# Attention passes of a graph network: columns of gathered rows made by ScalarE and TensorE out of a transposed table in SBUF

## The reference, cut to what matters

```python
h = (x @ W).reshape(-1, heads, out_ch)
alpha_s = (h * a_s[None]).sum(-1)
alpha_d = (h * a_d[None]).sum(-1)
e = alpha_s[src] + alpha_d[dst]          # the first also adds a term of edge_attr_8
e = jnp.where(e > 0, e, NEG_SLOPE * e)
w = jnp.exp(e - segment_max(e, dst)[dst])
out = segment_sum(w[:, :, None] * h[src], dst) / segment_sum(w, dst)
```

## Time and profile before

| | |
|---|---|
| median of the runs | 13222.6 us |
| span of the profiled execution | 13211.9 us |
| GpSimd busy | 9802.5 us (74%) |
| VectorE busy | 6811.8 us (52%) |
| ScalarE busy | 4061.7 us (31%) |
| TensorE busy | 517.1 us (4%) |

### The profile page before, as it was taken

How to read it: one execution, slowest core, us unless ns; L and a number is a source line. 1 busy time by engine, 2 the same in 40 slices (tenths; PEclk the granted TensorE clock), 3 DMA queues, 4 the chain that set the end, 5 groups by cost and what they waited for, 6 DMA issues and landing times. The chain is left out here.

```text
span 13211.9 us, 103483 instructions
## 1 busy us (share of the span) xinstructions
PE 517.1 (4%) x1768; PEld 338.5 (3%) x1768; DVE 6811.8 (52%) x10645; ACT 4061.7 (31%) x4014; POOL 9802.5 (74%) x10362
## 2 busy tenths in 40 slices
PE   3000001100000200000010000000000000000001
PEld 1000000100000200000000000000000000000000
DVE  2777876377777533333333333343333336656656
ACT  4333333233333311111111111111111113666663
POOL 7777776777777677777777777777777776777775
PEclk9999999555555655555555555555555555555555
DMA  8445444344444222222212222222222223444443
GB/s 334 120 123 129 123 123 107 90 123 123 123 122 124 64 66 65 63 65 66 63 45 61 61 63 62 60 49 58 62 61 61 61 63 89 160 160 156 162 160 116
DMA packets 977609, 1316.81 MB, mean 100 GB/s; under 512 B 660939, under 2 KB 676770, under 8 KB 963551
## 3 DMA queue, kind: packets, MB, share of 16 engines
q10 hardware_dynamic: 558595, 803.76, 18.8%
q0 software_dynamic: 334400, 373.85, 14.8%
q1 hardware_dynamic: 83996, 134.02, 2.8%
HBM read 651.23 MB, written 659.53 MB: 99 GB/s over the span
## 5 line engine op out<-in xcount | busy, mean ns | idle before, releaser
L1862 POOL DMA_INDIRECT c_y<-g_tab,srcs x4545 | 4291.3, 944 | 1386.9 <-issue 1386.9
L2318 POOL DMA_INDIRECT c_y<-h_tab,srcs x1547 | 1461.0, 944 | 506.4 <-issue 471.4
L824 POOL DMA_INDIRECT c_y<-h_tab,srcs x1531 | 1444.9, 944 | 467.1 <-issue 467.1
L824 POOL DMA_INDIRECT first_y<-h_tab,srcs x1452 | 1370.6, 944 | 445.2 <-issue 442.6
L1894 DVE TENSOR_TENSOR c_s<-c_y,c_ad 128x64 f32<-128x64 f32 x300 | 79.6, 265 | 1905.2 <-DMA c_y<-g_tab,srcs 1873.7
L1979 ACT ACTIVATE c_ex<-c_de 128x64 f32<-128x64 f32 x300 | 67.9, 226 | 3171.7 <-issue 2847.4
L1930 DVE COPY c_w_in<-c_ex 128x64 f32<-128x64 f32 x300 | 66.8, 223 | 1580.1 <-ACT c_ex L1979 1580.1
L1938 DVE TENSOR_TENSOR_SCAN c_acc<-c_r,c_w_in 128x1156 f32<-128x1156 f32 x300 | 753.9, 2513 | 10.4
L846 DVE TENSOR_TENSOR_SCAN c_q_all<-c_mask,c_q_in 128x408 f32<-128x408 f32 (+2 forms) x800 | 734.3, 986 | 16.3 <-issue 8.8
L890 DVE TENSOR_TENSOR_SCAN c_acc<-c_r,c_w_in 128x408 f32<-128x408 f32 (+2 forms) x800 | 732.0, 978 | 6.9
L939 ACT ACTIVATE c_q_in<-c_q_raw 128x1552 f32<-128x1552 f32 (+1 forms) x200 | 596.7, 2983 | 271.8 <-DVE c_q_in L906 197.5
(11 more groups left out here) (405 smaller groups left out, 6432.2 us busy)
## 6 DMA issues: line engine op xcount, KB each, us to landing
c_y<-g_tab SPq DMA_DIRECT2D x12288, 0.3 KB
rows_d<-c_row ACTq DMA_DIRECT2D x96, 2048.0 KB, 6.9
rows_d<-c_row ACTq DMA_DIRECT2D x288, 576.0 KB, 2.9
c_q_raw<-q_start ACTq DMA_DIRECT2D x194, 776.0 KB, 6.2
rows_d<-c_row ACTq DMA_DIRECT2D x192, 784.0 KB, 4.3
c_y<-h_tab SPq DMA_DIRECT2D x6144, 0.2 KB
c_y<-g_tab ACTq DMA_DIRECT2D x6144, 0.3 KB
q_start<-first_y SPq DMA_DIRECT2D x97, 776.0 KB, 8.9
```

Source lines behind the costliest of these rows:

```text
L824: nc.gpsimd.indirect_dma_start(y[:, g % NY, k, 0:D], None, h_tab, source(g, k))\
L1862: nc.gpsimd.indirect_dma_start(y[:, g % NY, k, :], None, g_tab, source(g, k))\
L2318: nc.gpsimd.indirect_dma_start(y[:, g % NY, k, :], None, h_tab, source(g, k))\
```

## The change

In the three attention passes ScalarE sends no single-row DMAs any more. Instead:

- The pass keeps `h` in SBUF turned: `turn_pairs` transposes it on TensorE two nodes of a partition at a time, `copy_pairs` writes it back over `h`. Column (pair, partition) then holds the 64 features of two neighbouring nodes.
- `scalar_part` copies, edge by edge, the column of an edge's source pair to a column of `xs`: 128 ScalarE copies of 128x1 for a column of `y`, in four parts of 32, the place of each read from registers. Two 16-bit places share a register, so a part loads 16 registers. ScalarE does this for four columns in six groups, halves before and behind `send`.
- `tensor_part` does the same for a fifth column in c4 and c5, by products of the identity with one column; `lift` copies the result from PSUM.
- `turn_rows` multiplies the 128 collected columns with the weights `wg` (kept in HBM by `keep_weights`), which gives both nodes' rows of 72, and VectorE's `choose` takes the one that is meant into `y`, by two masks.
- GpSimd gathers 90 of 96 columns in c3 and 89 in c4 and c5 (`pool_places`).
- The setup computes places and masks: some twenty small operations on VectorE, a transpose, two DMAs. `xs`, lists and masks lie over `ad_raw`.

```diff
+NITER, NPAIR = NGRP // NY, NC // 2
+Fetched = namedtuple("Fetched", "slot k on_scalar")
+FETCHED = [Fetched(2, 14, True), Fetched(3, 15, True), Fetched(4, 15, True), Fetched(4, 14, False),
+           Fetched(5, 14, True), Fetched(5, 13, False)]
+NF, NEARLY = len(FETCHED), 1
+BY_SCALAR = [f for f, c in enumerate(FETCHED) if c.on_scalar]
+BY_TENSOR = [f for f, c in enumerate(FETCHED) if not c.on_scalar]
+FROM_NF = ("rows_turned", "rows_chosen", "lifted_out")
+NSPOT, NMASK = NITER * NF, NITER * 2 * NF
...
+def pool_places(g, used):
+    kept = [SYNC_K] if g % NY in SYNC_SLOTS else []
+    kept += [FETCHED[f].k for f in used if FETCHED[f].slot == g % NY]
+    return [k for k in range(width(g)) if k not in kept]
...
+    spots_d = dram("spots_d", (NSPOT, P // 2), I32)
+    masks_d = dram("masks_d", (P, NMASK))
+    wg_d = dram("wg_d", (P, 2 * TG))
...
+    class ColumnFetch:
...
+        def turn_pairs(self, pe, banks):
+            for i, (c, n) in enumerate(BLOCKS):
+                if i >= 2:
+                    pe.wait_ge(*self.pairs_ready(i - 1))
+                    pe.nop(nofuse=True)
+                for j in range(n // 2):
+                    last = nc.tensor.transpose(banks[i % 2][:, j * P:(j + 1) * P],
+                                               h[:, c + 2 * j:c + 2 * j + 2, :].rearrange("p c f -> p (c f)"), ident[:])
+                last.then_inc(self.pairs_turned.h, 1)
+        def copy_pairs(self, act, banks):
+            for i, (c, n) in enumerate(BLOCKS):
+                act.wait_ge(*self.pairs_turned(i + 1))
+                act.activation(self.turned[:, c * D:(c + n) * D], banks[i % 2][:, 0:n * D], ACT.Copy)\
+                    .then_inc(self.pairs_ready.h, 1)
...
+        def load_early(self, act, n):
+            act.dma_start(self.at[0:NEARLY, 0:P // 2], spots_d[bass.ds(n * NF, NEARLY), :]).then_inc(self.early_at.h, 16)
+        def load_late(self, act, n):
+            act.dma_start(self.at[0:NF - NEARLY, P // 2:P], spots_d[bass.ds(n * NF + NEARLY, NF - NEARLY), :])\
+                .then_inc(self.late_at.h, 16)
+        def spots(self, engine, f, q):
+            row = self.at[f:f + 1, 0:P // 2] if f < NEARLY else self.at[f - NEARLY:f - NEARLY + 1, P // 2:P]
+            _, pairs = nc.values_load_multi_w_load_instructions(
+                row[:, q * NREG // 2:(q + 1) * NREG // 2], [engine], min_val=0, max_val=(NPAIR * P - 1) * 65537,
+                skip_runtime_bounds_check_because="columns of the turned table")
+            for pair in pairs:
+                yield (pair & 65535).with_bounds(min_val=0, max_val=NPAIR * P - 1)
+                yield (pair >> 16).with_bounds(min_val=0, max_val=NPAIR * P - 1)
...
+        def scalar_part(self, act, n, f, q):
+            at = self.scalars.index(f)
+            if q == 0:
+                act.wait_ge(*(self.early_at if f < NEARLY else self.late_at)(n * 16 + 16))
+                if not isinstance(n, int) or n * len(self.scalars) + at >= 2:
+                    act.wait_ge(*self.upto(self.rows_turned, n if at >= 2 else n - 1, self.scalars[at - 2]))
+                act.nop(nofuse=True)
+            for e, spot in enumerate(self.spots(mybir.EngineType.Activation, f, q), q * NREG):
+                last = act.activation(self.xs[at % 2][:, e:e + 1], self.turned[:, bass.ds(spot, 1)], ACT.Copy)
+            if q == NPART - 1:
+                last.then_inc(self.by_scalar.h, 1)
+        def tensor_part(self, pe, n, f, q):
+            if f not in self.tensors:
+                return
+            at = self.tensors.index(f)
+            if q == 0:
+                pe.wait_ge(*(self.early_at if f < NEARLY else self.late_at)(n * 16 + 16))
+                pe.nop(nofuse=True)
+                if not isinstance(n, int) or n:
+                    pe.wait_ge(*self.lifted_out((n - 1) * len(self.tensors) + at + 1))
+                    pe.nop(nofuse=True)
+            for e, spot in enumerate(self.spots(mybir.EngineType.PE, f, q), q * NREG):
+                last = nc.tensor.matmul(self.f_ps[at][:, e:e + 1], ident[:], self.turned[:, bass.ds(spot, 1)],
+                                        start=True, stop=True)
+            if q == NPART - 1:
+                last.then_inc(self.by_tensor.h, 1)
+        def lift(self, act, n, f):
+            if f not in self.tensors:
+                return
+            at = self.tensors.index(f)
+            act.wait_ge(*self.by_tensor(n * len(self.tensors) + at + 1))
+            if not isinstance(n, int) or n:
+                act.wait_ge(*self.upto(self.rows_turned, n - 1, f))
+            act.activation(self.xs[2 + at], self.f_ps[at], ACT.Copy).then_inc(self.lifted_out.h, 1)
+        def turn_rows(self, pe, n, f):
+            if f not in self.used:
+                return
+            if f in self.scalars:
+                x = self.xs[self.scalars.index(f) % 2]
+                pe.wait_ge(*self.by_scalar(n * len(self.scalars) + self.scalars.index(f) + 1))
+            else:
+                x = self.xs[2 + self.tensors.index(f)]
+                pe.wait_ge(*self.lifted_out(n * len(self.tensors) + self.tensors.index(f) + 1))
+            pe.nop(nofuse=True)
+            slot = FETCHED[f].slot
+            ago = [e for e in self.used if FETCHED[e].slot == (slot - 2 if slot > 3 else slot + 2)][-1]
+            if slot > 3 or not isinstance(n, int) or n:
+                pe.wait_ge(*self.upto(self.rows_chosen, n if slot > 3 else n - 1, ago))
+                pe.nop(nofuse=True)
+            nc.tensor.matmul(self.z[f], x, self.weights, start=True, stop=True).then_inc(self.rows_turned.h, 1)
+        def take_masks(self, v, n):
+            v.wait_ge(*self.masks_loaded(16))
+            if not isinstance(n, int) or n:
+                v.wait_ge(*self.upto(self.rows_chosen, n - 1, self.used[-1]))
+            v.tensor_copy(self.now, self.masks[:, bass.ds(n * 2 * NF, 2 * NF)]).then_inc(self.masks_taken.h, 1)
+            v.wait_ge(*self.masks_taken(n + 1))
+        def choose(self, v, n, slot, y, w):
+            here = [f for f in self.used if FETCHED[f].slot == slot]
+            if here:
+                v.wait_ge(*self.upto(self.rows_turned, n, here[-1]))
+            for f in here:
+                to, both = y[:, slot, FETCHED[f].k, 0:w], self.z[f]
+                half = both.shape[1] // 2
+                v.tensor_scalar(to, both[:, half:half + w], self.now[:, NF + f:NF + f + 1], None, ALU.mult)\
+                    .then_inc(self.rows_halved.h, 1)
+                v.wait_ge(*self.upto(self.rows_halved, n, f))
+                v.scalar_tensor_tensor(out=to, in0=both[:, 0:w], scalar=self.now[:, f:f + 1], in1=to,
+                                       op0=ALU.mult, op1=ALU.add).then_inc(self.rows_chosen.h, 1)
+                v.wait_ge(*self.upto(self.rows_chosen, n, f))
...
+                for f, c in enumerate(FETCHED):
+                    t = c.slot * GW + c.k
+                    last = v.tensor_copy(src_n[:, f:NSPOT:NF], srcs[:, t:NY * GW * NITER:NY * GW])
+                last.then_inc(vs.h, 1)
+                v.wait_ge(*vs.before("spot_near"))
+                v.tensor_scalar(spot_i[:], src_n[:], 1.0 / NC, 0.5 / NC - 0.5, ALU.mult, ALU.add).then_inc(vs.h, 1)
...
+                v.tensor_copy(spots[:], turned[0:NSPOT, P:2 * P]).then_inc(vs.h, 1)
...
+        def keep_weights(sp):
+            sp.wait_ge(*ch.upto(ch.names.index("put") + 1))
+            sp.dma_start(wg_d, wg[:].rearrange("p k f -> p (k f)")).then_inc(wg_stored.h, 16)
+            sp.wait_ge(*wg_stored(16))
...
-        taken = SYNC_SLOTS + [ACT_SLOT]
+        used = BY_SCALAR if bd is not None else [0, 1, 2, 4, 5]
+        taken = SYNC_SLOTS + [FETCHED[f].slot for f in used]
         gathered, by_sync = st.pass_slots(taken), SyncRows(st, y, g_tab, TG, 1)
-        at_read, act_got = st.dma("at_read", 16 * NACT), st.dma("act_got", 16 * P * NACT)
+        spare = ad_raw[:].rearrange("p t h -> p (t h)")
+        xs = [spare[:, n * P:(n + 1) * P] for n in range(2 + len(BY_TENSOR))]
...
-                    for k in range(by_pool(g, taken)):
+                    for k in pool_places(g, used):
...
+                def groups(n, more=True):
+                    score(n, 0)
+                    fetch.tensor_part(pe, n, 5, 0)
+                    score(n, 1)
+                    fetch.turn_rows(pe, n, 1)
+                    fetch.tensor_part(pe, n, 5, 1)
+                    score(n, 2)
+                    fetch.turn_rows(pe, n, 2)
+                    fetch.tensor_part(pe, n, 5, 2)
+                    score(n, 3)
+                    fetch.tensor_part(pe, n, 5, 3)
+                    score(n, 4)
+                    fetch.turn_rows(pe, n, 4)
+                    fetch.turn_rows(pe, n, 5)
+                    score(n, 5)
+                    if more:
+                        fetch.turn_rows(pe, n + 1, 0)
+                fetch.turn_pairs(pe, (pa, pb))
+                pe.wait_ge(*fetch.pairs_ready(NBLOCK))
+                pe.nop(nofuse=True)
```

(61 more changed lines are left out.)

132 lines of the change are left out of this document (106 added, 26 removed).

## The result

| | before | after |
|---|---|---|
| median of the runs | 13222.6 us | 14210.5 us (14207.9 to 14213.1) |
| ratio | | 1.0748, 95% interval 1.0717 to 1.0779 |
| profiled execution, span | 13211.9 us | 14211.4 us |
| pass c4, `g0` gather to last row store | 1900.5 us | 2226.0 us |

The kernel is 7.5% slower; I had forecast 13120 us in a range from 12990 to 13540. The step that failed is T, the spacing of ScalarE's copies: 0.150 us where the sum had 0.108.

The account below looks back on a forecast made before the run. GpSimd's gathers bound the kernel; the change would make ScalarE the bound by little. Passes c3, c4 and c5 would change by -15, -43 and -43 us, -101 in all: 13222.6 - 101 = 13120 us, range 12990 to 13540.

Parts of the forecast that it names:

- T: Spacing of ScalarE's 128x1 copies, register in the address: 0.108 us a copy, between 0.09 and 0.21.
- GpSimd bounds: GpSimd's gathers pace the attention passes at 1.249 us a column; 176 fewer save at most 220 us.
- The bound moves to ScalarE: ScalarE's round, 113.1 us in c4 and c5, 114.9 in c3, exceeds GpSimd's 111.2 and 112.4; chance 0.5.
- my list of signs: c4 rounds of 112 to 116 us, GpSimd idle until VectorE's product, loads 1.4 to 1.6 us, copies 0.10 to 0.12 apart.
- L: One load of 16 registers on ScalarE's queue: 1.5 us, between 1.0 and 3.14; four for each copied column.
- Rival 2: On ScalarE's queue loading 16 words costs much the same as 32; at 3.14 us the time is 14380 us; chance 0.21.
- 1.6 us for table load and loop: ScalarE's table load and loop in each round of an attention pass: 1.6 us.
- the 0.8 us: VectorE's `choose` in group 3, after a plain group, makes ScalarE wait 0.8 us a round.
- The start and end of a pass: ScalarE's loop begins 49 us in, last round 19.8 us shorter, last pieces 17 us: 47 us beside 16 rounds.
- Rival 3: A ScalarE copy with a register in its address costs 0.21 us: 52 us a round more, some 15600 us; chance 0.03.
- Rival 4: TensorE's fifth column comes late in c4 and c5, so ScalarE's `lift` waits; 10 us a round gives 13440; chance 0.04.
- Rival 1: GpSimd stays the bound: L and T together at least 2.6 us a round cheaper; 13003 us; chance 0.22.

## Why the prediction was wrong

- **GpSimd bounds, 1.249 us a column, 220 us at most to win:** right. The two runs with copies at 0.093 us took 214 and 215 us off, all four columns in place.
- **The bound moves to ScalarE:** right, by far more than I had it. I forecast 113.1 us for a round of c4 and 16 such rounds; it was 136.4 to 136.8. GpSimd's idle time ending at VectorE's product was on my list of signs.
- **T = 0.108 us:** the step that failed. "A register instruction on that queue takes 0.043 us and goes out beside the engine's work; two queue instructions of that size for each copy would be 0.09 us, the lower end." The queue holds more than the instructions' own time: with one short instruction of 37 ns a copy takes 97, so 60 ns come with every copy. And the unpacking needs three instructions for a pair, one of them with a division (73 ns), with 27 ns between the two that stand in line. Together 0.150 us a copy, 512 x 0.042 = 21.5 us a round. The list of full words, which changes only this and the number of loads, brought the spacing to 0.099. Within my bounds (0.09 to 0.21) I took the nearest row's value; that row had no register arithmetic, and the 60 ns stood in no row.
- **L = 1.5 us:** too high. 1.02, 7.7 us a round less. But a load behind the issue of a DMA is longer, and I knew of no such price though every row on ScalarE carried it. In the round shown the 16 loads take 21.4 us, 5.1 more than 16 x 1.02: 3.7 are the four straight behind a store of their own group, 1.0 is the first load of the column that follows the plain group's store (2.06 us), 0.4 the first loads of two other columns. Against my 24 us that leaves a gain of 2.6. Rival 2, that the load doesn't halve, is false: 1.02 and 1.97 us. The difference of 1 us between SyncE's and ScalarE's load of 32, on which I rested that rival, was the DMA ahead of it. I had read the Trainium skill's floor of about 600 ns ("DMA: Bandwidth & Descriptors", "Latency and other measured facts") as a fixed part under every load; these loads have no room for one: 2 x 1.02 - 1.97 leaves 0.07 us for what doesn't go by the count. As a shortest time it isn't tried here, since no load is below 1.0 us.
- **1.6 us for table load and loop:** 3.4 us short. From the branch to the next instruction of the queue pass 3.65 us in this round and 3.8 to 3.9 in most, against 0.23 in the kernel before. The length of the body beyond some point does not matter: between two branches ScalarE and its queue record 334 instructions in the kernel before, 600 with fixed columns (3.66 to 4.04 us in c4), 1058 with three packed columns (3.8) and 1384 in the change. The page's "instruction" queue moves 9.82 MB in place of 4.95. That a loop body over a certain length has to be fetched again at its head fits all of this, but no run had the same work in a short body: it stays argued.
- **The rest of the round.** Nine short pauses within the parts cost some 2.5 us (7542.93 to 7545.31 is one). They stand 87, 215, 471, 727, 855 and so on instructions behind the branch, always a multiple of 128 apart, in each of the five rounds of c4 counted, so they belong to the stream of instructions and not to a wait; this too fits fetching, and is not shown. VectorE's `choose` cost ScalarE less than the 0.8 us. 113.1 + 21.5 - 2.6 + 3.4 + 2.5 - 0.8 = 137.1 us, measured 136.4 to 136.8. T is nine tenths of the miss.
- **The start and end of a pass:** the first round began 53.5 us after the `g0` gather (7252.2 - 7198.7), forecast 49; 2226.0 - 16 x 136.6 = 40 us for both ends, forecast 47. The lists took 1.8 us from the first one's issue to the end of ScalarE's wait for it (7225.67 to 7227.51), where the sum had 3; column 0 took longer than its 19.8, as every column did.
- **Rival 3** (a copy with a register in its address costs 0.21 us) had the right engine and sign; the register in the address is free, what computes it isn't.
- **Rival 4:** false in the changed kernel (removing the column changed nothing), true in c4 and c5 as soon as ScalarE has a column less. Its price for the column was misread, too: the 2.26 us of the earlier trace rows are eight records but four products of the source, two records each, so 0.56 us a product and not 0.28. With one column a product takes 0.43, a column 4 x (13.8 + 1.11) = 60 us where I had 46, which was still hidden.
- **Rival 1:** at L = 1.35 it gains 16 x 0.15 = 2.4 us a round, not 2.6; nothing hangs on it.
- My last sentence named the condition, "if ScalarE's queue needs more than one register instruction between two copies". Rival 3, the nearest to it, had 0.03, and the sum left it out, although the source shows an `and` and a shift for each pair.

## What to carry to other kernels

Where an engine runs hundreds of tiny instructions, price its queue, not its data path: write down for each instruction the register instructions that its address needs (a mask or a shift isn't free, and may not fuse), 27 ns between two of these, some 60 ns for the instruction itself, and compare that sum with the spacing of the instructions alone (93 ns here). Packing two indices into a register to save loads pays only if the unpacking is cheaper than the load; here it was not, by 0.6 us in 32 copies. And when a bound is lifted, look for the engine whose queue order was written for the old pace: TensorE's column cost nothing until ScalarE's round became shorter.

## What the runs showed of the hardware

- Activations of 128x1 follow one another at 93 ns with fixed or ready addresses, at 97 to 99 with one register instruction of 37 ns each; at 134 and 166 ns, on average 150, where these take 73 ns or 35 and 43.
- As long as nothing is worked out between the copies, ScalarE's queue runs ahead of the engine, and a register load of 1.02 us between two parts leaves a break of 0.29 us from copy to copy.
- A fused register instruction takes 37 to 43 ns for times four plus base, 73 with a division ahead, 120 for multiply, subtract, multiply, add; a bitwise `and` stays an instruction of its own, 35 ns and 27 to the next.
- A register load takes 1.02 us for 16 and 1.97 us for 32 words on ScalarE's queue, 1.11 and 2.14 on TensorE's (medians), and straight behind the issue of the row store's DMA 1.88 and 2.92 on ScalarE's.
- The branch at the end of a loop costs ScalarE's queue 0.23 us with a body of 334 instructions and 3.65 to 4.04 us with 600 to 1384, in c4.
